# A graph kernel's attention scores: mask and linear part by TensorE in one PSUM bank, relu and running maximum joined on VectorE

## The reference, cut to what matters

```python
# attention layer, on h = relu(layernorm(x))
feat = (h @ W).reshape(N, HEADS, FOUT)
el = einsum('nhf,hf->nh', feat, attn_l); er = einsum('nhf,hf->nh', feat, attn_r)
e = leaky_relu(el[src] + er[dst], 0.2)
alpha = exp(e - segment_max(e, dst)[dst]) / its segment_sum
out = segment_sum(feat[src] * alpha, dst)          # then bias, layernorm, x + out
# each of three hops
h, t, rel = agg[head], agg[tail], edge_emb[edge_type]
att = sum((h @ q_w) * tanh((rel * t) @ k_w), axis=1)
w = segment_softmax(att, head)
agg = normalize(segment_sum(w * rel * t, head) / max(cnt, 1))
out = out + agg + entity_emb
```

## The kernel before

| engine | order in step k |
| --- | --- |
| PE | scores(k-5), transposes(k-7), sums(k-8) |
| ScalarE | exp(k-7), relu(k-5), fade's exp(k-7), copy(k-7) |
| VectorE | accumulate(k-9), fade(k-7), start_min(k-6), combine(k-6), masks(k-4), reduction(k-6) |
| GpSimd | gather(k), after `sum_ready` of k-7 |

## Time and profile before

### The profile page before, as it was taken

One profiled execution on the slowest core, in us unless ns is written; L12 is line 12 of the kernel. 1 busy time (PEld: TensorE's weight loads), 2 busy tenths in 40 slices (PEclk: granted clock), 3 DMA queues, 4 the chain that ended last, 5 costly groups with the idle time before them and its releaser, 6 DMA issues.

```text
span 9962.7 us, 287067 instructions
## 1 busy us (share of the span) xinstructions
PE 8791.4 (88%) x70817; PEld 7215.1 (72%) x70817; DVE 7908.6 (79%) x33588; ACT 7284.3 (73%) x23542; POOL 6843.0 (69%) x7059
## 2 busy tenths in 40 slices
PE   7992777788885999999997999999997999999997
PEld 7981666667674777777775777777775777777775
DVE  8884999999998777777776777777776777777776
ACT  1210999999997777777775777777775777777776
POOL 2331777777775777777775777777775777777775
PEclk9995999999998999999998999999998999999999
DMA  1002444444443555555556555555556555555556
GB/s 35 5 4 49 108 109 108 110 107 108 109 107 96 145 145 146 146 146 145 144 146 127 145 146 146 146 145 145 144 146 125 146 145 146 147 145 145 144 146 118
DMA packets 1110164, 1224.41 MB, mean 123 GB/s; under 512 B 452596, under 2 KB 847626, under 8 KB 1109740
## 3 DMA queue, kind: packets, MB, share of 16 engines
q1 hardware_dynamic: 863264, 752.80, 26.2%
q0 software_dynamic: 229008, 460.45, 21.3%
q10 hardware_dynamic: 17724, 9.01, 0.6%
HBM read 957.40 MB, written 260.45 MB: 122 GB/s over the span
## 4 chain that ended last, share of the span: by engine, by line
PE 43%; DMA 16%; issue 15%; DVE 10%; POOL 10%; ACT 4%; SPq 1%; DVEq 1%; POOLq 0%; ACTq 0%
PE bank L702 35%; DMA agg<-agg_d,arena 13%; POOL agg L670 9%; PE bank L855 3%; PE bank L840 3%; PE bank L808 2%; ACT arena L958 2%; DVE agg L1412 2%; DVE agg L1402 2%; DMA agg<-feat_d,arena 1%; DVE arena L1538 1%; ACT arena L1037 1%; DVE arena L1392 1%; DMA arena<-type_d 1%; DVE arena L1515 1%
## 5 line engine op out<-in xcount | busy, mean ns | idle before, releaser
L670 POOL DMA_INDIRECT agg<-agg_d,arena x5124 | 4862.8, 949 | 1752.4 <-issue 1520.6
L1538 DVE TENSOR_TENSOR arena<-agg,bank 128x256 f32<-128x256 f32 x2562 | 1077.9, 421 | 1547.9 <-DMA agg<-agg_d,arena 806.4
L670 POOL DMA_INDIRECT agg<-feat_d,arena x1708 | 1624.2, 951 | 565.1 <-issue 459.9
L702 PE MATMUL bank<-arena 128*128 128x129 f32 x10248 | 1822.4, 300 | 121.1 <-ACT arena L1037 109.0
L702 PEld LDWEIGHTS bank<-arena 128*128 128x128 f32 x10248 | 1341.1, 190 | 407.5 <-issue 155.8
L702 PE MATMUL bank<-tmp,wide 128*128 128x256 f32 x5124 | 1542.6, 383 | 0.5 <-DMA wide<-left_d 0.5
L1033 ACT ACTIVATE arena<-arena 128x1 f32<-128x1 f32 x2562 | 755.1, 295 | 1073.8 <-DVE arena L1376 1027.1
L702 PE MATMUL bank<-tmp,kw_s 128*128 128x256 f32 x5124 | 1536.6, 382 | 0.0
L1028 ACT ACTIVATE arena<-agg,arena 128x256 f32<-128x256 f32 x2562 | 1339.8, 523 | 15.1 <-DVE arena L1531 15.1
L702 PE MATMUL bank<-emb,arena 64*128 64x128 bf16 x15372 | 1302.1, 219 | 1.8 <-ACT wide L949 1.8
L1041 ACT ACTIVATE tmp<-bank 128x256 f32<-128x256 f32 x2562 | 985.6, 385 | 375.2 <-PE bank L702 299.5
(11 more groups left out here) (234 smaller groups left out, 15947.4 us busy)
## 6 DMA issues: line engine op xcount, KB each, us to landing
state_d<-arena SPq DMA_DIRECT2D x488, 455.0 KB
arena<-key_d SPq DMA_DIRECT2D x489, 448.0 KB
wide<-left_d SPq DMA_DIRECT2D x2562, 64.0 KB
arena<-type_d SPq DMA_DIRECT2D x367, 224.0 KB
agg<-agg_d,arena POOLq DMA_INDIRECT x5124
agg<-feat_d,arena POOLq DMA_INDIRECT x1708
arena<-er_d SPq DMA_DIRECT2D x854, 1.0 KB
arena<-peers SPq DMA_DIRECT2D x489, 7.0 KB
```

What stands on the lines that cost most here:

```text
L670: nc.gpsimd.indirect_dma_start(out=rows_r[:, k % R, c, 0:width], out_offset=None, in_=table, in_offset=bass.IndirectOffsetOnAxis(ap=peer_r ...
L702: return nc.tensor.matmul(out, lhsT, rhs, start=start, stop=stop)
L1538: V.tensor_tensor(val_r[:, j % R, :, 0:F], rows_r[:, j % R, :, 0:F], bank[0][:, 0:G].rearrange("p (c f) -> p c f", c=2), ALU.mult).then_in ...
```

## The change

- The attention bank now starts with a bf16 matmul of minus identity with the mask `off_r`, broadcast over both heads (512 columns), and the four transposes become four real f32 matmuls with `slope` (0.2 on the diagonal), added in the same bank. PE waits for `off_done` too, and for `min_done` of j-2 in place of `neg_done`.
- ScalarE's relu scales by 4 in place of 0.8 (the bank holds 0.2 el); where the mask stands its result is zero.
- VectorE's combine (L1402) goes. The fused reduction adds bank and relu, and keeps the running maximum, in `max_r` (`max_done`). In the next step, after accumulate, VectorE negates it to `min_r` and posts `min_done`. Signs of the meta columns follow.
- Peers have semaphores of their own, shared by both layers, and are loaded at k % 7 == 3 for the next unit, also across the end of a pipeline; the wait for `gathered` moves there from the unit's load. GpSimd waits for the peers alone.
- Relations: high and middle parts of the embeddings stand as one 128-row operand, with the one-hot matrix made twice (128 partitions; types are loaded to 128 partitions), the low part as a second matmul: two halves by two.
- Some constants and casts in setup.

```diff
@@ SP, load_store.step
+                    j = k - k % R + R
+                    if not b.last and k % R == PEERS_AT:
+                        if not (b.first and j < U):
+                            sp.wait_ge(q["gathered"][(j - R - 1) % R], b.landed("gathered", j - R - 1))
+                            apart(sp)
+                        at = peers[layer][:, 2 * j:2 * (j + R)] if b.first else peers[layer][:, bass.ds(2 * (b.at + j), 2 * R)]
+                        sp.dma_start(peer_r[:, j % U:j % U + R, :].rearrange("p a b -> p (a b)"), at).then_inc(q["peers"][j // R % 2], 16)
                     j = k
                     if not b.last and k % R == 0 and not (layer == 1 and b.first and k == 0):
                         if not b.first:
                             sp.wait_ge(q["off_done"], b.count(j - R - 1))
                             apart(sp)
-                            sp.wait_ge(q["gathered"][(j - R - 1) % R], b.landed("gathered", j - R - 1))
-                            apart(sp)
...
-                        sp.dma_start(flat(peer_r), at(peers[layer], 2)).then_inc(d, 16)
...
-                            sp.dma_start(flat(type_r)[0:RELS], row(type_d).partition_broadcast(RELS)).then_inc(d, 16)
+                            sp.dma_start(flat(type_r), row(type_d).partition_broadcast(P)).then_inc(d, 16)
@@ GpSimd, gather
-                    pool.wait_ge(q["unit"][k // R], b.landed("unit", k))
+                    pool.wait_ge(q["peers"][k // R], b.landed("peers", k))
@@ PE, attn_step
-                        pe.wait_ge(q["neg_done"], b.count(j - 2))
+                        pe.wait_ge(q["min_done"], b.count(j - 2))
...
+                    pe.wait_ge(q["off_done"], b.count(j))
+                    mm(bank[j % 2][:].rearrange("p (h e) -> p h e", h=HEADS), minus16[:],
+                       off_r[:, j % R, :].rearrange("p (o e) -> p o e", o=1).to_broadcast([P, HEADS, G]), True, False)
                     for h in range(HEADS):
                         for c in range(2):
-                            last = nc.tensor.transpose(
-                                bank[j % 2][:, h * G + c * P:h * G + (c + 1) * P],
-                                rows_r[:, j % R, c, h * (FH + 2) + FH + 1:h * (FH + 2) + FH + 2].to_broadcast([P, P]), ident[:])
+                            last = mm(bank[j % 2][:, h * G + c * P:h * G + (c + 1) * P],
+                                      rows_r[:, j % R, c, h * (FH + 2) + FH + 1:h * (FH + 2) + FH + 2].to_broadcast([P, P]), slope[:],
+                                      False, h == HEADS - 1 and c == 1)
                     last.then_inc(q["scores_ready"], 1)
@@ PE, hop_pe_step
-                        for i in range(3):
-                            last = mm(bank[0][:, c * P:(c + 1) * P], hot_r[0:RELS, j % R, c * P:(c + 1) * P], emb3[:, i, :], i == 0, i == 2)
+                        mm(bank[0][:, c * P:(c + 1) * P], hot_r[:, j % R, c * P:(c + 1) * P], emb_pair[:], True, False)
+                        last = mm(bank[0][:, c * P:(c + 1) * P], hot_r[0:RELS, j % R, c * P:(c + 1) * P], emb_low[:], False, True)
@@ VectorE, attn_step
                 j = k - 7
                 if b.has(j):
-                    fade(q, b, j, HEADS)
+                    dve.wait_ge(q["max_done"], b.count(j))
+                    V.tensor_scalar(min_r[:, j % R, :], max_r[:, j % R, :], -1.0, None, ALU.mult).then_inc(q["min_done"], 1)
+                    fade(q, b, j, HEADS, ALU.add)
                 j = k - 6
                 if b.has(j):
                     start_min(q, b, j, HEADS)
-                    dve.wait_ge(q["relu_done"], b.count(j))
-                    V.scalar_tensor_tensor(score_r[:, j % R, :], bank[j % 2][:], -SLOPE, relu_r[:, j % 2, :], ALU.mult, ALU.subtract).then_inc(q["neg_done"], 1)
...
                     for h in range(HEADS):
-                        last = V.tensor_tensor_reduce(out=score_r[:, j % R, h * G:(h + 1) * G], in0=score_r[:, j % R, h * G:(h + 1) * G],
-                                                      in1=off_r[:, j % R, :], scale=1.0, scalar=min_in_r[:, j % R, h:h + 1],
-                                                      op0=ALU.add, op1=ALU.min, accum_out=min_r[:, j % R, h:h + 1])
-                    last.then_inc(q["min_done"], 1)
+                        last = V.tensor_tensor_reduce(out=score_r[:, j % R, h * G:(h + 1) * G], in0=bank[j % 2][:, h * G:(h + 1) * G],
+                                                      in1=relu_r[:, j % 2, h * G:(h + 1) * G], scale=1.0, scalar=min_in_r[:, j % R, h:h + 1],
+                                                      op0=ALU.add, op1=ALU.max, accum_out=max_r[:, j % R, h:h + 1])
+                    last.then_inc(q["max_done"], 1)
```

More of the change, by code:

```diff
@@ L21 @@
 R = 7
+PEERS_AT = 3
 WINDOWS = -(-E // G)
@@ L88, in __init__ @@
         self.used = {name: value(BODIES * (U // ring) * inc, (U // ring) * inc) for name, (ring, inc) in uses.items()}
+        self.shared = 0 if hop is None else BODIES * 16
         self.uses = uses
@@ L100, in landed @@
         ring, inc = self.uses[name]
-        return self.used[name] + inc * (j // ring + 1)
+        return self.used[name] + inc * (j // ring + 1) + (self.shared if name in ("peers", "block") else 0)
 def pipeline(eng, hop, step, uses):
@@ L169, in gnn_kernel @@
         beta_s = sb("beta_s", [P, F])
-        emb_s = sb("emb_s", [RELS, F])
-        emb_rest = sb("emb_rest", [RELS, F])
-        emb3 = sb("emb3", [RELS, 3, F], BF16)
+        emb_s = sb("emb_s", [2 * RELS, F])
+        emb_rest = sb("emb_rest", [2 * RELS, F])
+        emb_high = sb("emb_high", [2 * RELS, F], BF16)
+        emb_pair = sb("emb_pair", [2 * RELS, F], BF16)
+        emb_low = sb("emb_low", [RELS, F], BF16)
+        rel_row = sb("rel_row", [2 * RELS, 1])
         qw_s = sb("qw_s", [P, F])
@@ L176, in gnn_kernel @@
         window_of = [sb(f"window_of{s}", [LANES, R], I32) for s in range(2)]
-        peers = [sb(f"peers{s}", [P, TILES], I32) for s in range(2)]
+        peers = [sb(f"peers{s}", [P, TILES + 2 * R], I32) for s in range(2)]
         lastg = [sb(f"lastg{s}", [P, NB], I32) for s in range(2)]
@@ L353, in gnn_kernel @@
         pipes_free = sem("pipes_free")
+        peers_loaded = [sem(f"peers_loaded{i}") for i in range(2)]
+        block_loaded = [sem(f"block_loaded{i}") for i in range(U)]
         pipes = []
@@ L357, in gnn_kernel @@
                 "unit": [sem(f"{q}unit_loaded{i}") for i in range(2)],
-                "block": [sem(f"{q}block_loaded{i}") for i in range(U)],
+                "peers": peers_loaded,
+                "block": block_loaded,
                 "gathered": [sem(f"{q}gathered{i}") for i in range(R)],
@@ L362, in gnn_kernel @@
                     "off_done", "min_in_done", "scores_ready", "min_done", "exp_done", "probT_ready", "probT_copied", "sum_ready",
-                    "acc_done", "fade_done") + (("relu_done", "neg_done") if q == "attn_" else (
+                    "acc_done", "fade_done") + (("relu_done", "max_done") if q == "attn_" else (
                         "rel_ready", "val_done", "valT_ready", "valT_copied", "right_ready", "right_done"))},
@@ L370, in apart @@
             eng.sem_inc(passed[eng.engine], 1)
-        uses = [{"unit": (U, 48), "block": (U, 16), "gathered": (R, 32), "stored": (U, 16)},
-                {"unit": (U, 64), "block": (U, 16), "gathered": (R, 32), "stored": (U, 16)}]
+        uses = [{"peers": (U, 16), "unit": (U, 32), "block": (U, 16), "gathered": (R, 32), "stored": (U, 16)},
+                {"peers": (U, 16), "unit": (U, 48), "block": (U, 16), "gathered": (R, 32), "stored": (U, 16)}]
         STORE = [10, 13]
@@ L391, in _ @@
             sp.dma_start(xs[0:NLAST, NB - 1, :], x[(NB - 1) * P:N, :]).then_inc(inputs_in, 16)
-            for a, d in ((w_s, w), (qw_s, q_w), (kw_s, k_w), (emb_s, emb)):
+            for a, d in ((w_s, w), (qw_s, q_w), (kw_s, k_w), (emb_s[0:RELS], emb), (emb_s[RELS:2 * RELS], emb)):
                 sp.dma_start(a[:], d).then_inc(inputs_in, 16)
@@ L467, in load_states @@
                         sp.dma_start(wide[:, b * SW:(b + 1) * SW], state_d[:, bass.ds(g * SW, SW)]).then_inc(state_in[part], 16)
+            sp.dma_start(peer_r[:, 0:R, :].rearrange("p a b -> p (a b)"), peers[0][:, 0:2 * R]).then_inc(peers_loaded[0], 16)
             pipeline(sp, None, load_store(0), uses[0])
@@ L1291, in _ @@
                 do(V.reduce_sum(wx[:, TW + h:TW + h + 1], junk[:], axis=AX))
[L1293 to L1297, removed]
+            do(V.tensor_copy(emb_high[:], emb_s[:]))
+            do(V.tensor_tensor(emb_rest[:], emb_s[:], emb_high[:], ALU.subtract))
+            do(V.tensor_copy(emb_pair[0:RELS], emb_high[0:RELS]))
+            do(V.tensor_copy(emb_pair[RELS:2 * RELS], emb_rest[RELS:2 * RELS]))
+            do(V.tensor_copy(emb_high[0:RELS], emb_rest[0:RELS]))
+            do(V.tensor_tensor(emb_s[0:RELS], emb_rest[0:RELS], emb_high[0:RELS], ALU.subtract))
+            do(V.tensor_copy(emb_low[:], emb_s[0:RELS]))
```

(10 more changed lines are left out.)

26 lines of the change are left out of this document (17 added, 9 removed).

## The result

The changed kernel takes 10673.45 us (median of 4 runs, 10672.22 to 10674.63), the kernel before 9965.74 in the same comparison: 1.071 times, interval 1.0692 to 1.0729. Forecast were 10685 us, in a range of 10540 to 10900.

A forecast was written before the change was run, and what follows sets the result against it. The prediction took GpSimd's gather issue as the bound, 2.50 us a group. From the profiled 9964.5 us, +732 (attention loop), -13.7 and -2.5 (peers) and +2 (setup) gave 10682, or 10685 as the timed median; range 10540 to 10900.

The forecast's parts named there:

- What bounds: Attention stage and hops: GpSimd's issue of gathers sets the pace, 2.50 us per group of 256 edges.
- The ring: Attention: PE's scores wait, through negation and accumulate, for PE's own last sums; 2.513 to 3.37 us a group, +732 us.
- scores with mask: Attention, PE: mask matmul 0.27 us plus eight f32 score matmuls 0.88, together 1.15 us of the loop.
- sums to accumulate: Attention: from PE's first matmul of the sums to the start of VectorE's accumulate, 1.15 us.
- to the negation: Attention, VectorE: from accumulate's start to the next operation's start, 0.40 us.
- back to PE: Attention: the negation's semaphore reaching PE, 0.05 us.
- Setup: Before the stages: a pass over 854 columns, a few casts and copies, two constants, +2 us.
- Peers: Own semaphore, earlier load: stalls before group 7 at hop starts go, -13.7 us; first gather earlier, -2.5 us.
- Pairs: Hops: six relation matmuls become four, 0.15 us less PE work a group, hidden under the gathers: 0 gain.
- Gathers staying the bound: Attention rival: the negation reaches PE without waiting for its last sums; total 9950 us, or 9920; chance 0.06.
- The shorter and the longer loop: Attention rivals: loop of 2.7 to 3.2 us, 10110 to 10540; or 3.6 to 4.0, 10880 to 11220; chance 0.08 each.
- The clock: Attention rival: each step's gap halves PE's clock, some 5.8 us a group, total about 12750 us; chance 0.03.

The follow-up runs named there:

- The run with the negation first: Changed kernel with VectorE's negation of group k-7 moved ahead of accumulate(k-9): 9958.05 us, 0.9986 of the kernel before.
- the doubled mask: Changed kernel with the negation moved ahead of accumulate, plus a second 512-column matmul by a zero matrix after the mask: 10026.84 us, 1.0069 of the kernel before.
- the run with the wait alone: Kernel before, with PE's scores waiting for fade_done of j-2 in place of neg_done: 10100.19 us, 1.0135 of the kernel before.
- the run with the waits swapped: Changed kernel with PE waiting for off_done first, then min_done: 13576.08 us, where the kernel before took 14144.94 in the same comparison.
- the peers' run: Kernel before with only the peers' own semaphores and earlier load: 9958.64 us, 0.9988 of the kernel before.
- no mask: Changed kernel without the mask matmul, attention scores unmasked: 10571.67 us, 1.0614 of the kernel before.

## Why the prediction was right

- **What bounds.** Right: GpSimd's gathers. The run with the negation first shows attention back at their pace with 0.7 us more PE work a group; the doubled mask shows where the cover ends, and that PE's work of a step, 2.38 us, was forecast well.
- **The ring.** Right in place and size: 3.39 us a step for 3.37 forecast, +726 us for +732. Its terms, forecast and measured: scores with mask 1.15, 1.12; transposes 0.42, 0.43; sums to accumulate 1.15, 1.04; to the negation 0.40, 0.39; the negation 0.15, 0.16; back to PE 0.05, 0.24. The terms as measured add up to 3.38, as forecast 3.32, to which 0.05 was added for a matmul's spacing and a wake-up. That the sum fits within 0.02 us is in part luck: the sums were 0.11 too long, the way back 0.19 too short. The sums' 1.15 was read from a single step; the run with the wait alone has 1.04 too (2503.67 to 2504.71). The way back left out that PE, once released, had another wait to check, worth 0.1 by the run with the waits swapped. In the run with the wait alone, where the released wait is the last one, it is 0.05 (2502.65 to 2502.70); the other 0.09 is not explained. Inside the first term the mask took 0.22 for 0.27, the eight f32 matmuls 0.89 for 0.88.
- **Not in the sum.** The attention pipeline's drain is longer by steps of 0.87 us: from the last gather to the first of the hops 123.3 us for 114.3, +9. Setup cost 5, not 2. The profiled executions differ by 710.1 us (10672.8 and 9962.7): 1.4 to the first gather, 726.1 in attention, 9.0 in the drain, -23.2 in the hops, -3.2 in the rest.
- **Peers.** The stalls at the hop starts went as forecast (14.6 us), but the term of -13.7 did not "count in full": the peers' run shows it given back, partly at the ends, partly by longer gathers. In the changed kernel the hops from first gather to the states' took 23 us less in all: 14.6 at the starts and 13.1 in the stalls near the ends, 12.0 by shorter gathers (4850.8 us for 4862.8), less 17.0 in longer waits for the states. The 25 us between it and the peers alone are mostly the gathers, 4850.8 for 4873.8 us, 4.5 ns each; the prediction took a gather's time as fixed, and why it moves no run here tests. Three more profiles of kernels with the same hops (negation first, no mask, two masks) have 10 to 27 us less than before, so single profiles scatter by as much as the term.
- **Pairs.** The total was right (0), the reason half wrong: 0.15 us less of PE's work was forecast, but four matmuls took 0.63 us where six took 0.43. PE's step in a hop rose from 2.38 to 2.48 us, and the forecast 0.90 busy was 0.994. It stayed hidden by 0.02 us.
- **Rivals.** Gathers staying the bound fell by the ring, and the run with the negation first gives its number, 9950 forecast, 9958 measured. The shorter and the longer loop fell by the step of 3.39 us. The clock stayed at 1.00 in the stage with PE 0.76 busy. The Trainium skill, TensorE: Matmul & The Clock Gate, Part 4: PE-mode transpose, says that transposes do not count as PE activity for the gate. The stage before, with half of its operations transposes, was granted 1.00 as well, so no run here tests that rule.

## What to carry to other kernels

Before a wait is moved to another semaphore, write down the order of each engine's program within a step and follow the wait back: if it leads through another engine to the last work of one's own step before, all that work becomes serial, and an edit that only seems to add 0.7 us of hidden work costs its full length and the way round. Moving one small instruction ahead of the one that waits undid 715 us. A bound found by idle times (0.30 us before every gather) told which savings are worth nothing, where busy shares and the chain pointed at PE. Check it against the length of the instruction itself: with the wait alone the idle time was still 0.31 us, and the gathers had grown from 949 to 1000 ns.

## What the runs showed of the hardware

- In a stretch with indirect gathers of one and the same row the 16 DMA engines were 0.99 busy at 66 GB/s; with 128 different rows they were 0.39 busy at 112 GB/s. Spreading the rows took 88 us off three hop ends.
- A bf16 weight load of 64 rows after one of 128, or the reverse, isn't done ahead: 0.15 us a matmul for 0.055 when all have 128 rows (4696.60 to 4696.76 for three). In the kernel before matmuls of 64 rows are 0.055 us apart as well (4601.59 to 4601.82 for four steps), and the next kind, of 128 rows, starts 0.15 us after the last of them.
- An f32 matmul of 128 columns that is first after a wait takes 0.1 us longer than the same behind another matmul (2504.12 to 2504.33, then 0.11 us each, in the run without the mask).
- The same indirect gather doesn't always hold GpSimd equally long: 946 ns on average in the first steps of the run with the wait alone, 1000 ns later in it. What lengthens it is not tested.
